# A mixture-of-experts stage: the second slot's loads, the rounding of the values and one weight transpose are put elsewhere in their queues

## The reference, cut to what matters

```
p = softmax(x @ gate_w.T); w, idx = top_k(p, 2); w = w / sum(w)
h = silu(x @ w1[e]) * (x @ w3[e])        # 512 -> 1024, for each expert e
y = h @ w2[e]                            # 1024 -> 512
out = sum over the two chosen experts of w * y
```

## Time and profile before

| | us |
|---|---|
| median of three runs (1570.58, 1570.87, 1576.12) | 1570.87 |
| the profiled execution's own time | 1562.95 |
| its span, first to last instruction | 1561.2 |
| busy: PE, DVE, ACT, POOL | 1284.3, 1343.4, 1097.9, 346.1 |

### The profile page before, as it was taken

How to read it: one execution, slowest core, us unless ns; L and a number is a source line. 1 busy time by engine, 2 the same in 40 slices (tenths; PEclk the granted TensorE clock), 3 DMA queues, 4 the chain that set the end, 5 groups by cost and what they waited for, 6 DMA issues and landing times.

```text
span 1561.2 us, 24670 instructions
## 1 busy us (share of the span) xinstructions
PE 1284.3 (82%) x8733; PEld 803.6 (51%) x8780; DVE 1343.4 (86%) x1868; ACT 1097.9 (70%) x1360; POOL 346.1 (22%) x401
## 2 busy tenths in 40 slices
PE   8993888888865689999999997477777777779787
PEld 3441455555543567788888885224343444444333
DVE  6998899999986799999989994798999999975963
ACT  5776778888853476777787773327898888882575
POOL 1113265555303654000000003001111111110440
PEclk9996999999987799999999999677787787879998
DMA  8996489788532899999999996699788888963001
GB/s 290 292 285 163 104 209 213 198 220 206 130 144 85 320 368 352 365 374 373 372 371 372 374 372 139 142 198 192 162 165 179 166 169 164 175 137 81 1 7 48
DMA packets 455153, 338.71 MB, mean 217 GB/s; under 512 B 368232, under 2 KB 370280, under 8 KB 454928
## 3 DMA queue, kind: packets, MB, share of 16 engines
q1 hardware_dynamic: 439488, 291.31, 66.7%
q0 software_dynamic: 11200, 37.76, 8.2%
q10 hardware_dynamic: 4368, 8.39, 1.4%
HBM read 205.86 MB, written 38.01 MB: 156 GB/s over the span
## 4 chain that ended last, share of the span: by engine, by line
PE 47%; DVE 32%; issue 9%; ACT 6%; DMA 3%; POOL 3%; POOLq 0%; DVEq 0%; ACTq 0%; SPq 0%
PE scores L1128 14%; DVE arena L2078 12%; PE bank L1161 8%; PE bank L1010 4%; PE scores L1229 4%; DVE wlo L1924 3%; PE scores L994 2%; DVE arena L1838 2%; ACT arena L1473 2%; PE scores L993 2%; PE bank L1276 2%; DVE arena L1824 2%; PE bank L1374 1%; POOL xs_d L857 1%; PE scores L1258 1%
## 5 line engine op out<-in xcount | busy, mean ns | idle before, releaser
L1924 DVE TENSOR_TENSOR wlo<-raw,whi 128x2048 fp32r<-128x2048 f32 x138 | 332.7, 2441 | 35.2 <-ACT whi L1526 35.2
L2078 DVE TENSOR_SCALAR_CACHE_REDUCE arena<-scores,arena 128x1024 f32<-128x1024 f32 x256 | 314.3, 1279 | 27.7 <-PE scores L1229 26.7
L1612 ACT ACTIVATE arena<-arena 128x2048 int16<-128x2048 f32 x128 | 273.5, 2148 | 74.4 <-POOL arena L893 37.8
L1526 ACT ACTIVATE whi<-raw 128x2048 fp32r<-128x2048 f32 x138 | 261.9, 1914 | 81.2 <-PE bank L1161 42.0
L1229 PE MATMUL scores<-arena 96*128 96x512 bf16 x512 | 191.1, 480 | 87.0 <-DVE arena L2078 82.0
L1128 PE MATMUL scores<-whi,xhi 128*128 128x512 f32 x368 | 150.3, 408 | 2.1 <-DVE xlo L1928 2.1
L1128 PE MATMUL scores<-whi,xlo 128*128 128x512 f32 x368 | 146.4, 398 | 0.0
L1128 PE MATMUL scores<-wlo,xhi 128*128 128x512 f32 x368 | 146.1, 397 | 0.0
L1473 ACT ACTIVATE arena<-scores 128x512 f32<-128x512 f32 (+3 forms) x256 | 116.6, 506 | 26.9 <-PE scores L994 26.9
L1824 DVE TENSOR_REDUCE arena<-scores 128x1 f32<-128x640 f32 (+3 forms) x128 | 127.6, 1017 | 4.0 <-PE scores L971 3.6
L1838 DVE TENSOR_TENSOR arena<-arena 128x1024 f16<-128x1024 f32 (+2 forms) x128 | 126.1, 1026 | 3.5 <-issue 1.8
(11 more groups left out here) (296 smaller groups left out, 2570.5 us busy)
## 6 DMA issues: line engine op xcount, KB each, us to landing
raw<-in_L_ffn_w SPq DMA_DIRECT2D x138, 1024.0 KB, 7.7
arena<-arena SPq DMA_DIRECT2D x32, 256.0 KB, 2.9
kst_d<-arena POOLq DMA_DIRECT2D x16, 384.0 KB, 5.2
tern_d<-arena POOLq DMA_DIRECT2D x24, 256.0 KB, 2.8
arena<-kst_d SPq DMA_DIRECT2D x16, 384.0 KB, 4.1
xs_d<-arena SPq DMA_DIRECT2D x23, 256.0 KB, 2.9
arena<-xs_d SPq DMA_DIRECT2D x22, 256.0 KB, 8.2
ys_d<-arena ACTq DMA_DIRECT2D x22, 256.0 KB, 6.9
```

Of the source, the lines that this page charges most:

```text
L1526: act.activation(whi[:, s % SPLITS], raw[:, s % RAWS], ACT.Copy).then_inc(hi_done, 1)
L1612: act.activation(dst, src, ACT.Exp, bias=ebias[n % SBUFS], scale=-1.0, accum_out=rsum[h % 2][:, t:t + 1]).then_inc(p_ready, 1)
L1924: dve.tensor_tensor(wlo[:, s % SPLITS], raw[:, s % RAWS], whi[:, s % SPLITS].bitcast(F32), ALU.subtract).then_inc(lo_done, 1)
L2078: dve.tensor_scalar(ssb[i][:, s:s + 1024], scores[:, s:s + 1024], nsq[:, h, t:t + 1], None, ALU.mult, ALU.min, accum_out=nmx[i][:, half:ha ...
```

## The change

- SP: the wait for `scattered` goes behind slot 1's pieces; slot 2's rows are loaded there too. Slot 1's rows are loaded by POOL, right behind its own wait for `scattered`, with a semaphore of their own.
- POOL: the values are rounded one tile (128 x 512) at a time in two alternating buffers; tile t waits for the first silu of slot 3+t, so 16 tiles stand in slots 3 to 18, three instructions each.
- SP: `turn_weights(0)` waits for all 16 gathers.
- PE: the transposes of the last slot's one-hot matrix stand behind the first half of slot 0's first product. ACT copies them after slot 0's rows and piece 2; DVE waits for them before it writes `wlo` of piece 2, whose place they occupy.

```diff
             load_piece(0, 5, 0)
-            sp.wait_ge(scattered, 16 * 2 * NT)
-            sp.dma_start(xsin[1], xs_d[P:2 * P, :]).then_inc(xs_loaded[1], 16)
             for u in range(1, SLOTS):
-                if u + 1 < SLOTS:
+                if 1 < u < SLOTS - 1:
                     load_rows(u + 1)
...
                 for i in range(4, 6):
                     load_piece(u, i, chosen[u])
-            sp.wait_ge(v_made, 3 * NC // 4)
+                if u == 1:
+                    sp.wait_ge(scattered, 16 * 2 * NT)
+                    load_rows(2)
+            sp.wait_ge(v_made, 3 * NC)
...
+            for s in gathered:
+                sp.wait_ge(s, 64)
             sp.wait_ge(h_turned, 2 * SLOTS)
             turn_weights(0)
...
             pool.wait_ge(scattered, 16 * 2 * NT)
-            pool.wait_ge(xs_turned, 1)
+            pool.dma_start(xsin[1], xs_d[P:2 * P, :]).then_inc(rows1_in, 16)
             pool.wait_ge(gw_turned, 1)
             pool.wait_ge(v_step, 2)
-            for g in range(NC // 4):
-                tiles = slice(4 * g, 4 * g + 4)
-                pool.dma_start(vchunk, v_d[tiles].rearrange("t p d -> p t d")).then_inc(v_back, 16)
-                pool.wait_ge(v_back, 16 * (g + 1))
-                pool.tensor_tensor(vchunk, vchunk, vinv..., ALU.mult).then_inc(v_made, 1)
...
+            pool.dma_start(vchunk[0], v_d[0]).then_inc(v_back, 16)
+            for t in range(NC):
+                v = vchunk[t % 2]
+                pool.wait_ge(v_back, 16 * (t + 1))
+                if t + 1 < NC:
+                    pool.dma_start(vchunk[(t + 1) % 2], v_d[t + 1]).then_inc(v_back, 16)
+                pool.wait_ge(silu_done, 2 * (V_SLOT + t) + 1)
+                pool.tensor_tensor(v, v, vinv, ALU.mult).then_inc(v_made, 1)
+                pool.wait_ge(v_made, 3 * t + 1)
+                pool.tensor_scalar(v, v, MAGIC, 1.0, ALU.add, ALU.mult).then_inc(v_made, 1)
+                pool.wait_ge(v_made, 3 * t + 2)
+                pool.tensor_scalar(vint[:, t], v, -MAGIC, 1.0, ALU.add, ALU.mult).then_inc(v_made, 1)
+                pool.wait_ge(v_made, 3 * t + 3)
...
-            up(0, 0)
+            up_half(0, 0, 0)
+            turn_last()
+            up_half(0, 0, 1)
...
                 if s == 2:
                     act.wait_ge(xs_turned, 1)
-                    act.wait_ge(oh_turned, 2)
...
+            round_slot(0)
+            round_piece(2)
             for g, bank in enumerate((bank4, bank5)):
                 act.wait_ge(oh_turned, g + 1)
                 act.activation(ohT[:, g * 512:(g + 1) * 512], bank[:, :], ACT.Copy).then_inc(ohT_ready, 1)
-            round_slot(0)
-            round_piece(2)
...
                 dve.wait_ge(hi_done, s + 1)
+                if s == 2:
+                    dve.wait_ge(oh_turned, 2)
```

More of the change, by code:

```diff
@@ L83 @@
 TERN_UNIT = 4
+V_SLOT = 3
 LN_APPLIED = (LN_STEPS + 2 * GT + 6, LN_STEPS + 4 * GT + 12)
@@ L360, in program @@
         grow = [gath.take(F32, D) for _ in range(2 * NT)]
-        vchunk = Region(chunk_at).take(F32, 4, D)
+        over_chunk = Region(chunk_at)
+        vchunk = [over_chunk.take(F32, D) for _ in range(2)]
         wT = [Region(WT_AT + w * 2 * FI * KC).take(BF16, FC, KC, P) for w in range(2)]
@@ L490, in program @@
         hi_done, lo_done = sem("hi_done"), sem("lo_done")
+        rows1_in = sem("rows1_in")
         xs_loaded = [sem(f"xs_loaded{a}") for a in range(2)]
@@ L682, in turn_weights @@
                 sp.dma_start_transpose(wT[w].rearrange("p o c n -> p (o c) n"), tern_d[w]).then_inc(wT_in, 16)
-            sp.wait_ge(h_turned, 2 * SLOTS)
-            turn_weights(0)
             def load_keys(h):
@@ L692, in load_queries @@
                 sp.dma_start(qhead[h % 2][0:K3, :], qst_d[h]).then_inc(k_loaded[h % 2], 16)
+            for s in gathered:
+                sp.wait_ge(s, 64)
+            sp.wait_ge(h_turned, 2 * SLOTS)
+            turn_weights(0)
             sp.wait_ge(moe_added, 3 * NT)
@@ L902, in _ @@
             pool.wait_ge(moe_added, 3 * NT)
-            pool.wait_ge(v_made, 3 * NC // 4)
+            pool.wait_ge(v_made, 3 * NC)
             stage_v(0, 0)
@@ L1105, in _, with turn_last @@
             ins.then_inc(xs_turned, 1)
[L1106 to L1110, removed]
+            def turn_last():
+                pe.wait_ge(r_step, R_LAST)
+                for g, bank in enumerate((bank4, bank5)):
+                    for t in range(4):
+                        ins = pe.transpose(bank[:, t * P:(t + 1) * P], ohl[:, 4 * g + t], idf)
+                    ins.then_inc(oh_turned, 1)
             def up_half(u, i, half):
@@ L1136, in turn_slot @@
             def turn_slot(u):
-                pe.wait_ge(xs_loaded[u % 2], 16 * ((u + 1) // 2))
+                if u == 1:
+                    pe.wait_ge(rows1_in, 16)
+                else:
+                    pe.wait_ge(xs_loaded[u % 2], 16 * ((u - u % 2) // 2))
                 pe.wait_ge(xlo_ready, u)
```

## The result

| us | before | after |
|---|---|---|
| median (lowest to highest) | 1570.72 (1565.27 to 1576.12) | 1547.82 (1547.45 to 1549.72) |
| profiled execution | 1562.95 | 1547.45 |
| its span | 1561.2 | 1545.7 |

The ratio is 0.9857, 95% interval 0.9822 to 0.9892: faster, by 22.9 us between the medians and by 15.5 between the profiled executions. Forecast were 1555.6 us and 1547.7 for the profiled execution.

What follows compares the result with a forecast made beforehand. PE was taken to bound the mixture stage, with four interruptions: slot 1's rows, early `wlo`, and the gathers among them. +6.4 - 6.5 - 10.4 + 3.2 - 8.0 = -15.3 us from 1570.87 gave 1555.6, range 1545 to 1566.

Steps and rivals of the forecast that it cites:

- Slot 1's rows: Early in slot 0: SP's early pieces slow the scatters and POOL's load, so rows land later, +6.4 us (-1 to +12.4).
- Start of slot 0: PE's first matmul comes 2.4 us earlier, but PE only reaches its wait for rows earlier: worth 0.
- Slot 0 after its rows: In slot 0, `hlo` comes 4.3 us earlier and the downward matmuls run 2.2 us faster: -6.5 us (-4.3 to -6.5).
- Slots 1 to 3: The three slots lengthened while POOL is busy return to 18.33 us each: -10.4 us (ends -8 and -10.4).
- Tiles: Slots 3 to 18: POOL's tile instructions may delay a critical `wlo`, 0.2 us by 16 tiles, +3.2 us (0 to 9.6).
- The tail: At the end, gathers without the transpose beside them land sooner: -8.0 us (ends -8.5 and -5).
- the offset: From profiled execution to median of the whole kernel: the median was taken to stand 7.9 us above.
- Fair turns: Rival for slot 1's rows: POOL's queue gets half, rows land at about 526, sum -20.3, 1550.6 us; chance 0.17.
- Starved scatters: Rival for slot 1's rows: scatters get a small share, rows at 537, sum -9.3, 1561.6 us; chance 0.13.
- POOL takes DVE's time: Rival for the tiles: each POOL instruction falls on a `wlo`, 2.05 us a slot, sum +14.3, 1585.2 us; chance 0.05.
- The tail gives nothing: Rival at the end: gathers are slow by themselves, sum -7.3, 1563.6 us; chance 0.05.
- Does not do what it says: Rival for the whole change: another wait stands behind each removed one, within 2 us of before; chance 0.02.

Runs made afterwards that it cites:

- e4: The changed kernel with PE, ACT and DVE in the old order at slot 0's start; median 1554.01 us.
- e5: The changed kernel with each tile released by DVE's first gate of its slot instead of by the first silu; 1554.65 us in one run.
- e11: e9 with DVE's scale arithmetic first and `wlo` of pieces 2 and 3 held until POOL has issued all 16 scatters; median 1543.81 us.
- e2: The kernel before with only the values' rounding changed to one tile a slot; median 1550.12 us.
- e14: e11 with each tile released by the end of the `wlo` in front of `hlo` instead of by the first silu; median 1537.33 us, ratio 0.9793.
- e8: The kernel before with only SP's wait moved behind slot 1's pieces and slot 1's rows loaded by POOL; 1574.19 us in one run.
- e3: The changed kernel without the wait for the gathers before the first weight transpose; median 1558.59 us.
- e1: The changed kernel, but SP still waits for all scatters before it asks for slot 1's pieces; median 1543.79 us.
- e13: e9 with slot 1's rows loaded by POOL instead of SP; 1546.71 us in one run.
- e9: The kernel before with the tiles and the transpose's wait for the gathers, without the change's other two parts; median 1544.51 us, ratio 0.9832.
- e12: e11 with DVE released once POOL has issued twelve of the 16 scatters; 1543.36 us in one run.

## Why the prediction was right, and where it was not

All differences are after minus before, from the table.

- **Slot 1's rows, +6.4 (-1 to +12.4).** Measured +8.0 (19.90 to 27.88): the size of the term was right within its ends, and so were two of its three parts. POOL's issue and load were put at 3.3 (0.3 + 0.8 + 5 - 2.77) and cost 3.1; the slower scatters were put at 3.2 and cost 3.1. The third, +1.8, is the next point. With `R_LAST` 3.2 us later in the second profile, PE's transposes at 535.79 are 532.6 on the old scale, in the 527 to 534 that was named.
- **Start of slot 0, 0.** This step failed. The earlier `xlo` came as said (507.94, right behind `R_LAST`). The `wlo` of piece 2 was put 0.8 us later than before and came 0.67 earlier (3.48 us after `R_LAST`, before 4.15), and "nothing PE needs soon" looked at PE alone. That `wlo` also decides which scatter's issue is stretched, and the scatters are what PE waits for: +1.8 for the rows (e4 against the change; 0.6 where the race went the other way, in e5), and +0.9 at the first store, which is not told apart. POOL's queue should have been read beside DVE's for those 10 us.
- **Slot 0 after its rows, -6.5.** Measured -6.76 (24.62 to 17.86 between the first two columns). Both halves came as said: PE's idle time in front of the downward products is 0.07 us instead of 4.30, and they take 5.81 instead of 8.04 (547.17, the chain of the kernel after).
- **Slots 1 to 3, -10.4.** Measured -10.34.
- **Tiles, +3.2 (0 to +9.6).** Measured -0.1. The mechanism was right, and e5 and e11 came near its upper end (+7.8 and +7.2). The mis-sized part is the length of POOL's instructions. The second was put at 0.45 us, a quarter of the 1.76 of a four times larger one, and takes 0.62; the hops of 0.09 us were right. So POOL's third, which was to start 0.17 us ahead of the `wlo` and cost it up to 0.3, started 0.05 us behind it and cost nothing. That margin was luck, not foresight: e11 loses it by 0.04 us. The ends 0 and 9.6 held both.
- **The tail, -8.0.** Measured -9.1 behind the last gather and +1.1 in their issue, -8.0 in all. That POOL's issue would take 1.1 us longer with DVE's adds beside it was not foreseen, nor that the gathers, 3.62 us to landing, would be faster than the 4.2 of the fastest one before.

The parts give -17.3 us in the stretch where -15.3 was forecast. The rest of the span gave +1.8 (3.2 later at `R_LAST`, 1.4 less behind the adds), in code that the change does not touch; so that the profiled execution came to 1547.45 against 1547.7 is luck: two sums, each 2 us off, in opposite directions.

The median was forecast 7.8 us too high. That step was the offset: before's profiled execution is 7.9 us under its median, and this was carried over as if it belonged to the program. After's is 0.4 under. Between medians the change gives 22.9 us, in the stretch 17.3. The other kernels show a larger gain between the medians than in the stretch too (e2 20.6 against 16.6; e14 33.4 or, against the runs beside it, 31.2 against 27.0), all but e4 (16.7 against 18.0). e8, without tiles and in one run, shows the same offset (3.5 slower against 8.5). It is that of the profiled execution of before, whatever is set against it; where in the program other executions of before lose the time, no trace shows. The record has the mean granted clock of each execution, and over the 30 others of before that ran beside the groups the longer ones tend to have the lower clock: 1564.96 to 1568 us at 0.902 to 0.907, 1572 to 1577 at 0.894 to 0.902. The profiled one had 0.905. That the clock makes all of the 7.9 us is not shown.

**The rivals.** *Fair turns*: the rows would have come 5 us before the forecast and came 1.6 after it. POOL's queue moved 2.36 of 7.96 MB in 508 to 530 us, 30%. The Trainium skill, DMA: Bandwidth & Descriptors, section on queues, rings and completion order, has queues served in turn while they have work. POOL's queue moved nothing up to 512 us. From 512 to 530, with a scatter between issue and landing all the time, it moved 2.36 of 7.30 MB, 32%, against the half worked out by the rule. Whether it had packets waiting at every DMA engine is not shown, so this speaks against the rule here without deciding it; the time that was worked out by it did not come. *Starved scatters*: not as far, +8.0 of +12.4, and of that only 3.1 are the scatters'. *POOL takes DVE's time*: the price is real (0.44 to 0.5 us a tile when POOL wins, against the 1.16 from which it would decide) and the change does not pay it. *The tail gives nothing*: out, by e3. *Does not do what it says*: half true of one part. The wait taken from SP bought nothing in any pairing; it cost 2.7 to 3.1 us at the rows and 0.8 (e1, not told apart) to 3.0 us (e13 against e4) in the stretch, and the change is faster in spite of it.

## What to carry to other kernels

When an edit moves an instruction that the bound engine doesn't wait for, look at what else that instruction locks out: here a VectorE operation with two SBUF inputs set when GpSimd could issue the scatters that everything waited for. Test the parts of a change one by one and in pairs: two of these four were worth 24.6 us and the other two took 7.35 of it back. Where an operation is free only because it loses a race by 0.05 us, release it by the end of what it must not disturb. And a quarter of a measured duration is not the duration of a quarter of the work.

## What the runs showed of the hardware that was not expected

- The issue of an indirect DMA on GpSimd, 0.96 us by itself, takes 1.9 to 3.03 us when it begins while a 128 x 2048 subtract of two SBUF operands runs on VectorE, and ends 0.83 us after that does (e9, e12, after). Begun ahead of the subtract, or with VectorE kept off (e11), each is 0.96.
- A 256 KB scatter lands 3.3 us sooner or later by what SP has queued: from the last issue's end to the last landing it took 2.0 us with SP waiting (e9, 521.97 to 523.97) and 5.3 with 1 MB loads in flight (after, 524.99 to 530.28).
- A DMA transpose of 2 MB held SP's queue for 8.01 us behind the gathers (after) and for 29.18 beside them (e3), and the last gather took 3.62 against 17.15.
- Two races of under 0.2 us between VectorE and GpSimd decided 1.2 us at the rows (after, e5) and 7.2 us over 16 slots (e9, e11).
